# Pairwise feature products on one core: vector, scalar and store programs written as loops, loads counted by GpSimd, the first loads issued by the store queue

## The reference

```python
i_idx, j_idx = jnp.triu_indices(f, k=1)
xw = jnp.einsum('bfe,ed->bfd', x, W)
return xw[:, i_idx, :] * x[:, j_idx, :]
```

## Time and profile before

| | |
|---|---|
| median of three runs | 655.6 us (655.19 to 655.65) |
| the profiled execution | 655.56 us, of which its span (first to last instruction) is 653.8 us |
| busy share of the span | VectorE 87%, TensorE 32%, ScalarE 16% |
| bytes moved by DMA | 277.00 MB, 424 GB/s over the span |
| the 38 slices between the first and the last of 40 | 403 to 437 GB/s, DMA engines at least 90% busy |
| last store issued; end of the span | 625.27 us; 653.8 us |

### The profile page before, as it was taken

One profiled execution on the slowest core, in us unless ns is written; L12 is line 12 of the kernel. 1 busy time (PEld: TensorE's weight loads), 2 busy tenths in 40 slices (PEclk: granted clock), 3 DMA queues, 4 the chain that ended last, 5 costly groups with the idle time before them and its releaser, 6 DMA issues.

```text
span 653.8 us, 3891 instructions
## 1 busy us (share of the span) xinstructions
PE 209.3 (32%) x1280; PEld 157.5 (24%) x1280; DVE 570.5 (87%) x544; ACT 101.8 (16%) x385; POOL 0.7 (0%) x6
## 2 busy tenths in 40 slices
PE   5936080805208052080520806134070613200000
PEld 4734060603206041060410605023050502200000
DVE  3999999999699996999879999998999999899920
ACT  3412030302103030030300303021030302100000
POOL 0000000000000000000000000000000000000000
DMA  8999999999999999999999999999999999999995
GB/s 333 403 432 433 435 437 432 431 435 417 427 435 434 434 427 432 435 433 435 417 432 432 435 435 433 434 435 433 433 432 435 423 427 429 435 435 435 431 427 239
DMA packets 10828, 277.00 MB, mean 424 GB/s; under 512 B 1344, under 2 KB 1344, under 8 KB 1344
## 3 DMA queue, kind: packets, MB, share of 16 engines
q1 hardware_dynamic: 9216, 260.05, 92.4%
q10 hardware_dynamic: 1600, 16.81, 6.3%
HBM read 16.81 MB, written 260.05 MB: 423 GB/s over the span
## 4 chain that ended last, share of the span: by engine, by line
DMA 60%; DVE 33%; issue 2%; PE 0%; ACTq 0%; DVEq 0%; ACT 0%
DMA out_dram<-out_ring 59%; DVE out_ring L196 33%; DMA x_sb<-in_x_dram 1%; ACTq L162 0%; PE xw_bank L123 0%; PE xT_ps L113 0%; DVEq L54 0%; ACT xw_sb L158 0%; DVEq L195 0%
## 5 line engine op out<-in xcount | busy, mean ns | idle before, releaser
L196 DVE TENSOR_TENSOR out_ring<-xw_sb,x_sb 128x256 f32<-128x256 f32 (+27 forms) x544 | 570.5, 1123 | 54.8 <-DMA out_dram<-out_ring 44.5
L123 PE MATMUL xw_bank<-W_sb,xT_sb 64*128 64x64 f32 x1024 | 138.9, 429 | 343.9 <-ACT xT_sb L153 341.9
L123 PEld LDWEIGHTS xw_bank<-W_sb,xT_sb 64*128 64x128 f32 x1024 | 118.1, 320 | 382.4 <-issue 355.7
L153 ACT COPY xT_sb<-xT_ps 128x256 f32<-128x256 f32 x128 | 48.1, 376 | 379.7 <-DVE out_ring L196 336.3
L113 PE MATMUL xT_ps<-identity,x_sb 128*128 128x128 f32 x256 | 83.7, 442 | 7.3 <-DMA x_sb<-in_x_dram 7.3
L158 ACT COPY xw_sb<-xw_bank 128x128 f32<-128x128 f32 x256 | 55.6, 270 | 74.3 <-PE xw_bank L123 74.3
L113 PEld LDWEIGHTS xT_ps<-identity,x_sb 128*128 128x128 f32 x256 | 39.4, 209 | 20.3 <-DMA x_sb<-in_x_dram 7.3
L153 ACT ACT_TABLE_LOAD x1 | 1.3, 1283 | 5.1 <-issue 5.1
L92 POOL TENSOR_SCALAR_AFFINE_SELECT identity<-identity 128x128 f32<-128x128 f32 x1 | 0.3, 294 | 0.2 <-POOL identity L90 0.2
L90 POOL MEMSET identity<- 128x128 f32 x1 | 0.2, 205 | 0.3 <-POOLq L209 0.3
L209 POOL MEMSET const-bfloat16-1.0<- 128x1 bf16 x1 | 0.1, 102 | 0.0
## 6 DMA issues: line engine op xcount, KB each, us to landing
out_dram<-out_ring SPq DMA_DIRECT2D x64, 3968.0 KB, 29.0
x_sb<-in_x_dram ACTq DMA_DIRECT2D x6, 2048.0 KB, 19.9
x_sb<-in_x_dram ACTq DMA_DIRECT2D x4, 1024.0 KB, 11.5
W_sb<-in_W_dram ACTq DMA_DIRECT2D x2, 16.0 KB, 2.1
```

The costliest lines, as they stand in the source:

```text
L123: last = nc.tensor.matmul(xw_ps[g % 2][odd][:, m, :], xT_sb[g % 2][rows, m, :], W_sb[rows, :], start=True, stop=True)
L153: nc.scalar.copy(xT_sb[g % 2][:], xT_ps[g % 2][:]).then_inc(xT_copied, 1)
L196: last = nc.vector.tensor_tensor(slot[:, place:place + n, :], xw_sb[t % 2][:, i:i + 1, :].to_broadcast([LANES, n, E]), x_sb[buf][:, r, j:j ...
```

## The change

VectorE's program becomes a loop over laps and, within it, a loop over the four loads of a lap, with two tiles in its body; the place in `x_sb` (now one tensor of eight tiles) is taken from a register, and so are the counts that it waits for. ScalarE's program becomes two tiles written out, a loop of four passes over two tiles that ends with one late load, and a loop of three passes. SyncE's stores become a loop of eight passes over two tiles. The first four loads (five DMAs) are issued by SyncE, ahead of the stores and on their queue, no longer by ScalarE behind the loads of `W`. GpSimd waits for each load and adds its tiles to one counter, `tiles_landed`, on which TensorE and VectorE wait. `stored`, `chunk_ready` and `late_landed` are raised at the start, so that the first passes of the loops find them satisfied.

```diff
-        x_sb = [sb(f"x_sb{n}", [LANES, ROWS, F, E]) for n in range(XBUFS)]
+        x_sb = sb("x_sb", [LANES, LAP, F, E])
...
+            pool.wait_ge(first_landed, 16)
+            pool.sem_inc(tiles_landed, 1)
+            for g in range(XBUFS):
+                pool.wait_ge(x_landed[g], 16)
+                pool.sem_inc(tiles_landed, ROWS if g > 0 else ROWS - 1)
+            for g in range(XBUFS, LOADS):
+                pool.wait_ge(late_landed, 16 * (g - XBUFS + 2))
+                pool.sem_inc(tiles_landed, ROWS)
...
+            for slot in range(CHUNKS):
+                sp.sem_inc(stored[slot], 16)
+            sp.dma_start(x_sb[:, 0], x_loads[0, :, 0]).then_inc(first_landed, 16)
+            sp.dma_start(x_sb[:, 1:ROWS], x_loads[0, :, 1:ROWS]).then_inc(x_landed[0], 16)
+            for g in range(1, XBUFS):
+                sp.dma_start(x_sb[:, g * ROWS:(g + 1) * ROWS], x_loads[g]).then_inc(x_landed[g], 16)
+
+            with sp.Fori(0, LOADS) as g:
+                for r in range(ROWS):
+                    for c in range(CHUNKS):
+                        sp.wait_ge(chunk_ready, XW_BUFS * CHUNKS + (g * ROWS + r) * CHUNKS + c + 1)
+                        sp.dma_start(out_tiles[g, r, :, c * CHUNK * E:(c + 1) * CHUNK * E],
+                                     out_ring[c][:]).then_inc(stored[c], 16)
...
+            with act.Fori(0, LOADS - XBUFS) as g:
+                for buf in range(XW_BUFS):
+                    tile((g + 1) * XW_BUFS + buf, buf)
+
+
+                act.wait_ge(late_landed, 16 * (g + 1))
+                act.dma_start(x_sb[:, bass.ds(g * ROWS, ROWS)], x_loads[g + XBUFS]).then_inc(late_landed, 16)
+            with act.Fori(LOADS - XBUFS + 1, TILES // XW_BUFS) as k:
+                for buf in range(XW_BUFS):
+                    tile(k * XW_BUFS + buf, buf)
...
+            dve.sem_inc(chunk_ready, XW_BUFS * CHUNKS)
+            with dve.Fori(0, TILES // LAP) as lap:
+                with dve.Fori(0, XBUFS) as u:
+                    for r in range(ROWS):
+                        tile(lap, u, r)
```

More of the change, by code:

```diff
@@ L62, in sem @@
             return ctx.enter_context(nc.semaphore(name))
-        x_sb = [sb(f"x_sb{n}", [LANES, ROWS, F, E]) for n in range(XBUFS)]
-        xw_sb = [sb(f"xw_sb{n}", [LANES, F, E]) for n in range(2)]
+        x_sb = sb("x_sb", [LANES, LAP, F, E])
+        xw_sb = [sb(f"xw_sb{n}", [LANES, F, E]) for n in range(XW_BUFS)]
         out_ring = [sb(f"out_ring{n}", [LANES, CHUNK * E]) for n in range(CHUNKS)]
@@ L76, in pairwise_interaction_kernel @@
         identity_ready = sem("identity_ready")
-        x_landed = [[sem(f"x_landed{n}_{r}") for r in range(ROWS if n == 0 else 1)] for n in range(XBUFS)]
+        x_landed = [sem(f"x_landed{n}") for n in range(XBUFS)]
+        late_landed = sem("late_landed")
+        first_landed = sem("first_landed")
+        tiles_landed = sem("tiles_landed")
         transposed = sem("transposed")
@@ L93, in _, with transpose_group @@
                                     base=0, pattern=[[-1, LANES]], channel_multiplier=1).then_inc(identity_ready, 1)
+            pool.wait_ge(first_landed, 16)
[6 more added lines that the diff above has]
+                pool.sem_inc(tiles_landed, ROWS)
         @block.sync
         def _(sp):
[L97 to L102, removed]
-            for slot in range(CHUNKS):
-                sp.wait_ge(stored[slot], 16 * TILES)
+            for slot in range(CHUNKS):
+                sp.sem_inc(stored[slot], 16)
[10 more added lines that the diff above has]
+            for slot in range(CHUNKS):
+                sp.wait_ge(stored[slot], 16 * (TILES + 1))
         @block.tensor
         def _(pe):
-            def transpose_group(buf, r, g):
+            def transpose_group(place, g):
                 for m in range(HALF):
                     f = g * GROUP + 2 * m
-                    two = x_sb[buf][:, r, f:f + 2, :].rearrange("p f e -> p (f e)")
+                    two = x_sb[:, place, f:f + 2, :].rearrange("p f e -> p (f e)")
                     last = nc.tensor.transpose(xT_ps[g % 2][:, m, :], two, identity[:])
@@ L128, in _ @@
             pe.wait_ge(W_landed, 32)
[L129 to L139, removed]
+            with pe.Fori(0, TILES // LAP) as lap:
+                for place in range(LAP):
+                    t = lap * LAP + place
+                    pe.wait_ge(tiles_landed, t + 1)
+                    transpose_group(place, 0)
+                    for g in range(GROUPS):
+                        if g + 1 < GROUPS:
+                            transpose_group(place, g + 1)
+                        project_group(t, g)
         @block.scalar
         def _(act):
[L143 to L149, removed]
             def copy_xT(t, g):
@@ L153, in copy_xT, with copy_xw, tile @@
                 nc.scalar.copy(xT_sb[g % 2][:], xT_ps[g % 2][:]).then_inc(xT_copied, 1)
-            def copy_xw(t, g):
+            def copy_xw(t, buf, g):
                 act.wait_ge(projected, t * GROUPS + g + 1)
                 for odd in range(2):
-                    nc.scalar.copy(xw_sb[t % 2][:, g * GROUP + odd:(g + 1) * GROUP:2, :],
+                    nc.scalar.copy(xw_sb[buf][:, g * GROUP + odd:(g + 1) * GROUP:2, :],
                                    xw_ps[g % 2][odd]).then_inc(xw_copied, 1)
[L161 to L167, removed]
-                copy_xT(t, 0)
[L169 to L175, removed]
+            def tile(t, buf):
+                copy_xT(t, 0)
+                act.wait_ge(chunk_ready, (t + 1) * CHUNKS)
                 for g in range(GROUPS):
@@ L178, in _, with tile @@
                         copy_xT(t, g + 1)
-                    copy_xw(t, g)
+                    copy_xw(t, buf, g)
+            for odd in range(2):
+                act.dma_start(W_sb[odd * E:(odd + 1) * E, :], W).then_inc(W_landed, 16)
+            act.sem_inc(xw_copied, XW_PRIME)
+            act.sem_inc(late_landed, 16)
+            for buf in range(XW_BUFS):
+                tile(buf, buf)
+            with act.Fori(0, LOADS - XBUFS) as g:
[4 more added lines that the diff above has]
+            with act.Fori(LOADS - XBUFS + 1, TILES // XW_BUFS) as k:
+                for buf in range(XW_BUFS):
+                    tile(k * XW_BUFS + buf, buf)
         @block.vector
         def _(dve):
-            for t in range(TILES):
-                load, r = divmod(t, ROWS)
-                buf = load % XBUFS
+            def tile(lap, u, r):
+                place = u * ROWS + r
+                t = lap * LAP + place
+                dve.wait_ge(tiles_landed, t + 1)
+                x_tile = x_sb[:, bass.ds(place, 1)].rearrange("p t f e -> p (t f) e")
                 for c in range(CHUNKS):
-                    if t > 0:
-                        dve.wait_ge(stored[c], 16 * t)
+                    dve.wait_ge(stored[c], 16 * (t + 1))
                     slot = out_ring[c][:].rearrange("p (q e) -> p q e", e=E)
-                    for i, j, n, place in chunks[c]:
-                        if i == 0 and r < len(x_landed[buf]):
-                            dve.wait_ge(x_landed[buf][r], 16 * (load // XBUFS + 1))
+                    for i, j, n, at in chunks[c]:
                         if i % GROUP == 0 and j == i + 1:
```

5 lines of the change are left out of this document (3 added, 2 removed).

## The result

The changed kernel takes 657.07 us (656.9 to 657.65) against 655.62 us (655.01 to 655.79) of the kernel before: ratio 1.0025, with a 95% interval from 1.0017 to 1.0033. It is slower by 1.45 us, where 1.6 us less was forecast. The profiled execution took 657.03 us with a span of 655.2 us.

What follows compares the result with a forecast made beforehand. The prediction took the DMA byte stream to bound the kernel: its start, its fullness and how evenly its 16 engines finish. Terms: 655.56 - 0.96 - 0.4 - 0.2 = 654.0 us, range 650.5 to 658.0.

Steps and rivals of the forecast that it cites:

- rival (b): End of the kernel: the tail of two or three late DMA engines evens out, 651 us; chance 0.14.
- Steps 1 and 2: Start: first loads on SyncE's queue, no longer behind W, -0.96 us; loads and stores in one queue, -0.4 us.
- step 2: At 20 to 30 us: loads and stores in one queue instead of two, -0.4 us, bounds 0 and -0.84.
- Step 3: Instruction fetches on the DMA engines: fewer packets beside the data, -0.2 us, bounds 0 and -2.2.
- Step 4: VectorE's loop: 40 new sequencer instructions a tile hidden under running multiplications, 0; 3.8 us a tile is free.
- step 6: ScalarE's late loads: none is late, 0, bounds plus and minus 0.8 us; SyncE's register instructions are covered.
- Step 5: GpSimd's counter: first tile reaches TensorE some 0.2 us later than the load allows, still earlier than before; 0.
- Rival (c): Loops fetch their code again at jumps, queueing packets on a DMA engine on the path: 658 to 661 us; chance 0.12.
- Rival (d): VectorE becomes the bound if register instructions are not hidden and cost 0.15 us each: 689 us; chance 0.04.

Runs made afterwards that it cites:

- v1: The kernel before with only the first five loads issued by SyncE ahead of the stores, no loops or counter: 653.62 us.
- a1: The changed kernel with the first five loads back on ScalarE's queue behind W, all else as changed: 658.58 us.
- m3: The kernel before with a counting loop of 2,048 passes added on the idle GpSimd, on which nothing waits: 664.50 us.
- v2: v1 with W twice on the diagonal of a 128x128 block, so fewer TensorE matmuls and ScalarE copies: 651.18 us.
- a2: The changed kernel with VectorE's program written out for 16 tiles, without its loop and register instructions: 655.76 us.
- a5: The changed kernel with each late load issued within ScalarE's loop ahead of its second tile's copies, as many instructions: 656.85 us.

## Why the prediction was wrong

*What bounds the kernel* was right: the stream of bytes, and within it the start, the fullness and the last engine to finish. That the tail of two or three late engines was the largest single loss was seen, but what makes an engine late was left to rival (b), as a thing that might even out.

*Steps 1 and 2* were right in kind, and in the size of their sum. The issue moved to 0.99 us (1.02 forecast), and undoing the move costs 1.5 us (0.96 + 0.4 forecast). The reason weighed for step 2, two queues, holds for the smaller part of the dip alone: v1 has none of it, with a later first store. The Trainium skill ("DMA: Bandwidth & Descriptors", Issuing engines are not separate DMA queues) says that DMAs of all issuing engines run on the same 16 engines and interleave. The traces agree in the main: a1 with two queues (394 GB/s) and the changed kernel with one (408) both had the dip, and v1 with one queue (439) had none.

*Step 3* can't be judged. There were 9 instruction packets for 12, and a gain of 0.2 us is less than these runs tell apart.

*Step 4 is the step that failed.* It priced VectorE's 40 new sequencer instructions a tile by VectorE's own time and took 0 because they are hidden. On VectorE they nearly are: some 0.15 us a tile shows, far less than the 3.8 us a tile that it said was free. (One reading there was wrong, without harm: the 0.71 us at 75.18 do not lie between two tiles, for the next tile's first multiplication starts at 81.05 us.) But executed instructions cost the DMA engine that ends last some 2.2 ns each, on the engines tested (m3: 8.9 us for 4,097 on GpSimd; v2: 2.4 for 1,150 on TensorE and ScalarE; a2: 1.3 for 665 on VectorE). The change executes 1,056 more: 666 on VectorE, 220 on SyncE, 147 on ScalarE, 23 on the others. That is 2.3 us that stood in no term, neither in step 4 nor in step 6, where SyncE's register instructions were taken as covered.

The sum now: a1, which has the whole change but the place of the first loads, is 2.9 us slower than the kernel before; the count explains 2.3 us of that. Moving the loads takes 1.5 us off, and +1.45 was measured. The remaining 0.6 us is not settled; the late loads' place (a5) may hold 0.2 of it. The landings of the last store say the same in another way: 15 engines 1.1 us earlier, one engine's lag 2.5 us longer.

*Step 5* was right: VectorE's first multiplication starts at 10.04 us, before 10.23, although GpSimd stands between. *Step 6* was right on the late loads, as far as a5 shows.

*Rival (c)* had the sign and the place, one late DMA engine, but not the mechanism. The loops do not fetch their code again at each jump: fewer packets ran. The Trainium skill ("Runtime: NRT & Kernel Launch", Instruction fetch mechanics) says that a taken branch to a target outside a window of two pages forces a fetch. By that rule and the 9 packets these loops stay within it; no run here measured the window. Rival (d) is refuted, and rival (b) was half true: the tail can shrink, by executing less.

What the 2.2 ns are was not shown. It goes with the count of executed instructions and with the time in which they run, not with code, bytes or waits. One candidate is the record of each instruction, on which every trace rests. The Trainium skill ("NOTIFIC — Programmer's Manual", The life of a record) says that trace records of 16 bytes are written over AXI to a ring in memory; 2.2 ns at one DMA engine's 27 GB/s would be 59 bytes, an estimate of about four such records. No run here shows that these writes share a path with a DMA engine. Each timed execution came with a span too, so whether one without any record pays the same is open.

## What to carry to other kernels

When DMA bandwidth is the bound, look at the last few microseconds engine by engine (the DMA share in windows of 2 us): one engine of 16 that ends late is paid in full, whatever the mean rate says. In such a kernel an instruction is not free because its engine is idle: count executed instructions in the page's first line, and prefer one large instruction to two, which here gave more than any other single edit. (All these executions were recorded ones.) And take only the part of a change that pays: the five loads moved alone gave 0.3%, the loops around them took it back and more.

## What was not expected of the hardware

One executed instruction costs the last DMA engine about 2 ns, on GpSimd as on VectorE and, together, TensorE and ScalarE: 8.9 us for 4,097 additions and jumps that nothing waits for, all of it while they run. A store cut into 120 and 8 lanes ran at 206 GB/s with the engines 95% busy, where one of 128 lanes runs at 430. And with a first store at 18.92 us, while the loads still ran, the rate was 30 GB/s lower over ten microseconds than with one at 20.39.
